# A graph network on one core: column sums of the tail tiles moved into relations, loads moved into the choice, w2 scaled earlier

## The reference

```python
x = x + _L1_gnn_ref(_layernorm(x), L1_gnn_weight, edge_weight1, src, dst, edge_type_16)
x = x + _L1_ffn_ref(_layernorm(x)[None], Wr, br, W1, b1, W2, b2, gamma, beta)[0]
```

```python
logits = jnp.mean(x, axis=1) @ Wr + br          # x: the normed rows, mean over all 6250
... softmax, capacity scale, softmax, top_k(2), softmax of the two
out = w_a * y_a + w_b * y_b                     # y_e = gelu(x W1_e + b1_e) W2_e + b2_e
out = _layer_norm(out + x, gamma, beta)
```

## Time and profile before

| | |
|---|---|
| median of three executions | 3174.28 us (3172.42 to 3178.28) |
| the profiled execution | 3175.51 us, span 3173.8 us |
| mean granted TensorE clock | 0.886 of full speed |
| TensorE busy | 2449.2 us, 77% |
| VectorE busy | 1760.3 us, 55% |
| GpSimd busy | 1947.8 us, 61% |
| ScalarE busy | 850.3 us, 27% |

### The profile page before, as it was taken

One profiled execution on the slowest core, in us unless ns is written; L12 is line 12 of the kernel. 1 busy time (PEld: TensorE's weight loads), 2 busy tenths in 40 slices (PEclk: granted clock), 3 DMA queues, 4 the chain that ended last, 5 costly groups with the idle time before them and its releaser, 6 DMA issues. The chain is left out here.

```text
span 3173.8 us, 37270 instructions
## 1 busy us (share of the span) xinstructions
PE 2449.2 (77%) x8964; PEld 1576.1 (50%) x8964; DVE 1760.3 (55%) x4135; ACT 850.3 (27%) x1683; POOL 1947.8 (61%) x1900
## 2 busy tenths in 40 slices
PE   4537999999999999999979918999999300004897
PEld 3425566656665666565546505666666200003565
DVE  6776555555556666666640046665555544543664
ACT  2211333333333333333223303333333100002221
POOL 6477555646666777778830057777777777760443
PEclk9767999999999999999989958999999755555999
DMA  7553544445445555555531374555554433332210
GB/s 251 119 172 89 152 136 129 142 148 146 139 143 158 150 148 159 168 159 150 147 98 67 111 257 145 157 152 169 155 156 142 124 105 104 106 98 86 77 56 29
DMA packets 241629, 428.29 MB, mean 135 GB/s; under 512 B 49866, under 2 KB 132418, under 8 KB 241538
## 3 DMA queue, kind: packets, MB, share of 16 engines
q0 software_dynamic: 84608, 232.41, 27.6%
q1 hardware_dynamic: 131250, 171.29, 15.8%
q10 hardware_dynamic: 25680, 23.60, 2.2%
HBM read 271.16 MB, written 155.97 MB: 135 GB/s over the span
## 5 line engine op out<-in xcount | busy, mean ns | idle before, releaser
L810 POOL DMA_INDIRECT gat_rows<-h_table,idx x799 | 901.4, 1128 | 424.5 <-issue 231.3
L1437 POOL DMA_INDIRECT rel_rows<-transformed,rel_idx x799 | 756.0, 946 | 475.3 <-issue 466.5
L1054 PE MATMUL bank<-tr_wr,tr_xt 128*128 128x512 f32 x1568 | 724.0, 600 | 39.1 <-ACT tr_row L903 34.3
L1054 PEld LDWEIGHTS bank<-tr_wr,tr_xt 128*128 128x128 f32 x1568 | 293.4, 191 | 328.9 <-issue 277.6
L1019 PE MATMUL bank<-mo_xt,mo_w 128*128 128x256 f32 (+1 forms) x1600 | 431.8, 393 | 15.2 <-ACT mo_ht L894 13.5
L1626 DVE SCALAR_TENSOR_TENSOR bank<-rel_rows,rel_now,bank 128x256 f32<-128x256 f32 x823 | 403.1, 490 | 40.3
L903 ACT ACTIVATE tr_row<-bank 128x512 f32<-128x512 f32 x392 | 233.8, 597 | 675.8 <-PE bank L1054 662.6
L1037 PE MATMUL bank<-mo_w,mo_ht 128*128 128x256 f32 x1568 | 369.3, 381 | 4.5 <-ACT mo_ht L894 4.5
L1019 PEld LDWEIGHTS bank<-mo_xt,mo_w 128*128 128x128 f32 x1600 | 286.9, 192 | 148.0 <-issue 101.4
L1209 DVE TENSOR_TENSOR gat_rows<-gat_rows 128x1024 f32<-128x1024 f32 (+1 forms) x169 | 254.5, 1529 | 156.2 <-DVEq L1200 156.2
L1037 PEld LDWEIGHTS bank<-mo_w,mo_ht 128*128 128x128 f32 x1568 | 299.1, 191 | 55.5 <-issue 11.0
(11 more groups left out here) (295 smaller groups left out, 2342.2 us busy)
## 6 DMA issues: line engine op xcount, KB each, us to landing
transformed<-tr_row SPq DMA_DIRECT2D x392, 256.0 KB, 2.2
ys<-ex_y ACTq DMA_DIRECT2D x160, 128.0 KB, 2.2
gat_rows<-h_table,idx POOLq DMA_INDIRECT x799
rel_rows<-transformed,rel_idx POOLq DMA_INDIRECT x799
ex_w<-L_ffn_W SPq DMA_DIRECT2D x16, 512.0 KB, 12.2
h_table<-hrow SPq DMA_DIRECT2D x49, 132.0 KB, 2.4
records<-xa SPq DMA_DIRECT2D x49, 132.0 KB
x_moved<-tr_x SPq DMA_DIRECT2D x24, 256.0 KB, 3.2
```

The costliest lines, as they stand in the source:

```text
L810: pool.indirect_dma_start(out=rows[:, column(u, j), :], out_offset=None, in_=p.h_table[:], in_offset=bass.IndirectOffsetOnAxis(ap=idx[u][: ...
L1054: ins = pe.matmul(p.bank[6 + c % 2][:], xt2[:, k, u * P:(u + 1) * P], wr[:, k, m * CW:(m + 1) * CW], start=(k == 0), stop=(k == KD - 1))
L1437: pool.indirect_dma_start(out=rows[:, column(u, j), :], out_offset=None, in_=p.transformed[:], in_offset=bass.IndirectOffsetOnAxis(ap=idx[ ...
```

## The change

Three things are moved, and some names and counts follow.

1. The column sums of the tail tiles leave `choose_two` and stand in `relations`, behind TensorE's last group. VectorE signals `rows_done` after every pair of tail tiles and after the last tile (15 signals); TensorE waits for it tile by tile, and at the end for its own `summed_up`. The sums lie in banks 1 and 2 in place of 0 and 1.
2. SP loads gamma and beta and, for the first two done batches, `xd` and `x3` in `choose_two`, and waits there until all six have landed. The buffers are kept ones now. In `feed_forward` the expert weights are issued first, then b2, then only `ye` for these two batches. For later batches `xd` and `x3` are issued ahead of `ye`.
3. `scale` stands ahead of batch 0, behind the two operations on b2.

FREE, REUSED and X_LOADS have the values 9, 29 and 32, so the loads of `rec` in `relations` are the same as before.

```diff
@@ relations, SP, TensorE and VectorE @@
-    FREE = TAIL - DONE
+    FREE = max(TAIL - DONE, 0)
+    REUSED = DONE + FREE
+    X_LOADS = 32 if FREE else 16
...
             group(GROUPS - 1, True)
+            for t in range(TAIL):
+                pe.wait_ge(rows_done, t // 2 + 1)
+                for k in range(KD):
+                    ins = pe.matmul(p.bank[1 + k][:, 0:1], p.rec[:, t, k * P:(k + 1) * P], p.ms[:, DONE + t, 2:3],
+                                    start=(t == 0), stop=(t == TAIL - 1))
+            ins.then_inc(summed_up, 1)
+            pe.wait_ge(summed_up, 1)
...
                 spread_of(i, 2 * i, 2)
+                if tail:
+                    dve.sem_inc(rows_done, 1)
...
             spread_of(PAIRS, NT - 1, 1)
+            dve.sem_inc(rows_done, 1)
@@ choose_two @@
             sp.dma_start(br[:], a["L1_ffn_br"].rearrange("(o e) -> o e", o=1)).then_inc(w_in, 16)
+            for n, name in enumerate(("L1_ffn_gamma", "L1_ffn_beta")):
+                sp.dma_start(p.gb[:, n], bass.AP(tensor=a[name].tensor, offset=0, ap=[[0, P], [1, D]])).then_inc(ahead, 16)
+            for g in range(2):
+                sp.dma_start(p.xd[g][:], p.xn_table.rearrange("(g j q) d -> g q j d", q=P, j=G)[g]).then_inc(ahead, 16)
+                sp.dma_start(p.x3[g][:], p.x_moved.rearrange("(t q) d -> q t d", q=P)[:, g * G:(g + 1) * G, :]).then_inc(ahead, 16)
+            sp.wait_ge(ahead, 16 * 6)
...
-            for t in range(TAIL):
-                for k in range(KD):
-                    ins = pe.matmul(p.bank[k][:, 0:1], p.rec[:, t, k * P:(k + 1) * P], p.ms[:, DONE + t, 2:3],
-                                    start=(t == 0), stop=(t == TAIL - 1))
-            ins.then_inc(summed, 1)
...
-            dve.wait_ge(summed, 2)
+            dve.wait_ge(summed, 1)
@@ feed_forward @@
             for n, e in enumerate(experts):
-                sp.dma_start(b2[:, n], a["L1_ffn_b2"][bass.ds(e, 1)].broadcast_to([P, D])).then_inc(b_in, 16)
-            for n, name in enumerate(("L1_ffn_gamma", "L1_ffn_beta")):
-                sp.dma_start(gb[:, n], bass.AP(tensor=a[name].tensor, offset=0, ap=[[0, P], [1, D]])).then_inc(b_in, 16)
-            for n, e in enumerate(experts):
...
+            for n, e in enumerate(experts):
+                sp.dma_start(b2[:, n], a["L1_ffn_b2"][bass.ds(e, 1)].broadcast_to([P, D])).then_inc(b_in, 16)
...
                         sp.wait_ge(finished, units(b - 1))
+                        sp.dma_start(xd[s][:], xns[g]).then_inc(loaded[s], 16)
+                        sp.dma_start(x3[s][:], moved[:, g * G:(g + 1) * G, :]).then_inc(loaded[s], 16)
                     for n, e in enumerate(experts):
                         sp.dma_start(ye[s][n][:], ys[bass.ds(e, 1), g].rearrange("o q j d -> (o q) j d")).then_inc(loaded[s], 16)
-                    sp.dma_start(xd[s][:], xns[g]).then_inc(loaded[s], 16)
-                    sp.dma_start(x3[s][:], moved[:, g * G:(g + 1) * G, :]).then_inc(loaded[s], 16)
...
-            dve.wait_ge(b_in, 16 * 4)
+            dve.wait_ge(b_in, 16 * 2)
...
-                if b == 1:
+                if b == 0:
                     scale()
```

More of the change, by code:

```diff
@@ L1327, in relations @@
     LOCAL = E1 * F
-    FREE = TAIL - DONE
-    assert DONE % 2 == 0 and FREE >= 0
+    FREE = max(TAIL - DONE, 0)
+    REUSED = DONE + FREE
+    X_LOADS = 32 if FREE else 16
+    assert DONE % 2 == 0
     with p.phase() as ctx:
@@ L1403, in _ @@
             sp.dma_start(beta[:], bass.AP(tensor=a["L1_ffn_beta"].tensor, offset=0, ap=[[0, P], [1, D]])).then_inc(beta_in, 16)
-            sp.dma_start(p.rec[:, FREE:TAIL, :], moved[:, 0:DONE, :]).then_inc(x_in[0], 16)
-            sp.dma_start(p.rec[:, 0:FREE, :], moved[:, DONE:TAIL, :]).then_inc(x_in[0], 16)
+            sp.dma_start(p.rec[:, FREE:REUSED, :], moved[:, 0:DONE, :]).then_inc(x_in[0], 16)
+            if FREE:
+                sp.dma_start(p.rec[:, 0:FREE, :], moved[:, DONE:REUSED, :]).then_inc(x_in[0], 16)
             for e in range(E1):
@@ L1408, in _ @@
                 sp.dma_start(w2[:, e * F:(e + 1) * F, :], a["L1_ffn_W2"][e].rearrange("(f q) d -> q f d", q=P)).then_inc(w_in[2 * e // E1], 16)
-            sp.wait_ge(x_in[0], 32)
+            sp.wait_ge(x_in[0], X_LOADS)
             for t in range(DONE):
@@ L1412, in _ @@
                 sp.dma_start(moved[:, t, :], x3b[t % 2][:]).then_inc(x3_out[t % 2], 16)
-            for g in range(GROUPS):
+            for g in range(-(-(NT - REUSED) // G)):
+                lo, hi = g * G, min((g + 1) * G, NT - REUSED)
                 sp.wait_ge(xn_ready, g + 1)
-                sp.dma_start(p.rec[:, FREE + g * G:FREE + (g + 1) * G, :],
-                             moved[:, TAIL + g * G:TAIL + (g + 1) * G, :]).then_inc(x_in[1], 16)
+                sp.dma_start(p.rec[:, FREE + lo:FREE + hi, :], moved[:, REUSED + lo:REUSED + hi, :]).then_inc(x_in[1], 16)
                 sp.wait_ge(x_in[1], 16 * (g + 1))
-                sp.sem_inc(tail_ready, G)
+                sp.sem_inc(tail_ready, hi - lo)
         @block.gpsimd
@@ L1694, in spread_of @@
                 dve.sem_inc(x3_done, 1)
-            dve.wait_ge(x_in[0], 32)
+            dve.wait_ge(x_in[0], X_LOADS)
             for u in range(2):
@@ L1701, in pair @@
                 if reused:
-                    dve.wait_ge(tail_ready, 2 * i + 2 - TAIL)
+                    dve.wait_ge(tail_ready, 2 * i + 2 - REUSED)
                     p.alone(dve)
@@ L1707, in pair @@
                 spread_of(i, 2 * i, 2)
-            for lo, hi, tail, reused in ((0, DONE // 2, False, False), (DONE // 2, TAIL // 2, True, False), (TAIL // 2, PAIRS, True, True)):
+                if tail:
+                    dve.sem_inc(rows_done, 1)
+            for lo, hi, tail, reused in ((0, DONE // 2, False, False), (DONE // 2, REUSED // 2, True, False), (REUSED // 2, PAIRS, True, True)):
+                if lo == hi:
+                    continue
                 with dve.Fori(lo, hi) as i:
                     pair(i, tail, reused)
-            dve.wait_ge(tail_ready, DONE)
+            dve.wait_ge(tail_ready, NT - REUSED)
             tile(PAIRS, 0, NT - 1, NT - 1 - DONE, True)
             spread_of(PAIRS, NT - 1, 1)
+            dve.sem_inc(rows_done, 1)
             for u in range(2):
@@ L1737, in choose_two @@
                                         "exp_ready", "exp_done", "pair_ready", "spread_done"))
+        ahead = p.sem("two_ahead")
         block = ctx.enter_context(nc.Block())
@@ L1841, in feed_forward @@
         BATCHES.append(("tail", n))
+    assert BATCHES[0] == ("done", 0) and BATCHES[1] == ("done", 1)
     with p.phase() as ctx:
@@ L1876, in units, with landed @@
             return sum(size(*BATCHES[i]) for i in range(b))
-        def loads(b):
-            return sum(1 for i in range(b) if BATCHES[i][0] == "done" and i % 2 == b % 2)
+        def landed(b):
+            return sum(4 if i >= 2 else 2 for i in range(b + 1) if BATCHES[i][0] == "done" and i % 2 == b % 2)
         def loads_of(b):
@@ L1918, in base @@
                     s = b % 2
-                    pool.wait_ge(loaded[s], 16 * 4 * (loads(b) + 1))
+                    pool.wait_ge(loaded[s], 16 * landed(b))
                     for j in range(G):
@@ L2042, in _ @@
                 s, n = b % 2, size(kind, g)
-                if b == 1:
+                if b == 0:
                     scale()
                 if kind == "done":
-                    dve.wait_ge(loaded[s], 16 * 4 * (loads(b) + 1))
+                    dve.wait_ge(loaded[s], 16 * landed(b))
                 for j in range(n):
@@ L2083, in build @@
         attention(p)
-        p.rec = p.keep("rec", [P, TAIL, D], F32)
+        p.rec = p.keep("rec", [P, max(DONE, TAIL), D], F32)
         relations(p)
+        p.gb = p.keep("gb", [P, 2, D], F32)
+        p.xd = [p.keep(f"xd{n}", [P, G, D], F32) for n in range(2)]
+        p.x3 = [p.keep(f"x3{n}", [P, G, D], F32) for n in range(2)]
         choose_two(p)
```

7 lines of the change are left out of this document (3 added, 4 removed).

## The result

The changed kernel takes 3140.68 us (median of 4; 3139.08 to 3144.52), the kernel before 3173.35 (median of 4 on its chips, the three shown above and one more). The ratio is 0.9897, 95% interval 0.988 to 0.9914: 32.7 us faster, with 3144.5 forecast and 3139 to 3151 given as range. The profiled execution took 3144.52 us, the slowest of the four, with a span of 3142.7 against 3173.8: 31.1 us less, with 29.8 forecast. That it took the very time that was forecast for the median is chance. Two of the runs further down hold one execution each, of 5962.09 and 6845.3 us, that stands far outside all others, and their medians are given without it.

The account below looks back on a forecast made before the run. TensorE's tail groups bound the end, behind two holes: column sums standing alone after 385.7 us idle, and a 5.5 us wait for w2. +1.0 - 22.2 - 5.5 - 3.1 = -29.8 us from 3174.28 gives 3144.5, range 3139 to 3151.

Parts of the forecast that it names:

- The sums: End of relations: column sums hide in TensorE's idle time, only the last tile's 4 passes show, +1.0 us.
- I gave it 0.03: Rival in relations: the sums aren't hidden, all 116 passes run in a row after it, 3168.4 us; chance 0.03.
- The choice: Stage choose_two: without the sums, SP's wait for the early loads ends it at 12.0 us; -22.2 us.
- VectorE's part: In the choice: products wait for the small loads wr and br until 2.8, so VectorE ends at about 10.3 us.
- The start of the last stage: Weights issued 2.05 us earlier gain nothing, since TensorE waits for ScalarE's 29 norms and copy of b1.
- Half clock: Start of the last stage: TensorE's half-speed start stays, until about 9 us after its first transposes.
- Scaling and clock: First two groups: early scaling removes the wait for w2, -5.5 us; without that pause the clock stays full, -3.1 us.
- VectorE now scales w2 ahead of batch 0 ... the 5.5 us go: Last stage: scaling ends near 2927 or 2930, TensorE asks at 2945.8, so the second group's wait vanishes, -5.5 us.
- The prefetch did hold the choice: Rival in the choice: early loads move at the slow rate and the choice ends at 16.7, 3149.2 us; chance 0.07.
- the slow case: In the choice: the 2.36 MB move at 181 to 190 GB/s, the choice ends at 16.7 us, gain -17.5; chance 0.07.
- The wait for w2: Rival in the last stage: scaling is delayed past the first group, 5.5 and 3.1 us stay, 3153.1 us; chance 0.04.
- half clock after 385 us: Rival in the last stage: idle TensorE stays at half clock, slower, at most 3354 us; chance 0.02.

Follow-up runs that it names:

- the kernel with 5 norms later: Against the changed kernel, ScalarE norms the last 5 of 29 tail tiles in the first group's time, behind the copy of b1: 3143.2 us, ratio 0.99.
- an experiment of its own: Six useless products on TensorE inside its wait for w2, against the kernel with only the sums moved: 3148.23 us against 3151.62.
- the two kernels that take one part away: Changed kernel with scaling again behind batch 0: 4041.32 and 4035.4 us; with early loads back in the last stage: 4034.05 and 4033.94 us.

## Why the prediction was right, point by point

**The sums.** Forecast +1.0 for the end of relations, measured +1.06 (2.91 against 1.85). That they hide was right on the chip the forecast was made for; the two other chips show a condition that I hadn't weighed: TensorE's expert groups must be through before the last tail tiles are. With 385.7 us to spare I gave it 0.03, which is fair for the chip of the profile and says nothing of a chip on which TensorE itself pauses.

**The choice.** Forecast -22.2, measured 13.12 - 35.47 = -22.35. The loads landed where the two later batches said: by 11.8 us (13.12 less the 1.32 of the barriers) against 12.0. The rule of the Trainium skill that I weighed against them (page "DMA: Bandwidth & Descriptors", section "Anatomy of one DMA — SWDGE (gpsimd) path") would have had them at 8.3, an estimate worked out from its fit, and the choice ended by VectorE; the trace decides against this reading of it. One term was mis-sized, off the path: VectorE's part was 9.69 and not 10.3, because wr and br didn't hold anything. The products with wr, which wait for both loads, started 0.15 us behind VectorE (0.14 before), and 1.96 us after wr's issue, 1.54 after br's, so both had landed by then; the 2.4 us that I took from a 16 KB load were too much for br.

**The start of the last stage.** Forecast nothing, measured 14.47 and 14.47: the norms covered the earlier weights, as the kernel with 5 norms later shows. Half clock: 20.0 us for the first group before, without its wait for w2, and 19.46 after (2923.12 - 2903.66), because the clock rose 8 us after the first transposes and not 9. In stretches (columns as above), 0.62 as the mean of 2911 to 2912 puts the rise a quarter from its end:

```profile
2911.00:2912.00 1.00, 1.00 (x3) 0.37 (x2) 1.00 (x2) 0.38 (x1) 1.00 (x2) 0.62 0.00 0
2922.00:2924.00 2.00, 2.00 (x11) 1.15 (x10) 1.96 (x6) 0.97 (x2) 1.46 (x2) 1.00 0.20 70
```

Over the runs that don't wait for w2 the first group takes between 18.56 and 19.98. That half microsecond was in the range, not in the sum.

**Scaling and clock.** Forecast -5.5 and -3.1, measured: no wait, and 29.87 against 32.85 in the second group. The sizes were right, and the second has an experiment of its own. The step "VectorE now scales w2 ahead of batch 0 ... the 5.5 us go" was right in its sum and wrong in whom it credits: I named both that the scaling moves and that the batches run some 5 us earlier by the loads, and charged the whole gain to the first. Either nearly suffices. On the chip of the forecast this rests on the lengths of the last stage, which are the same on all chips: the two kernels that take one part away ran on the others only.

**The sum.** -29.8 forecast; by these lengths -30.3 (79.83 against 110.09 us from the last copy to the third group), and 0.8 us by which VectorE's last copy happened to come earlier, 31.1 in all. The median went 32.7 down; the rest is the spread between executions, of which the profiled one was the slowest.

**The other rivals.** The prefetch did hold the choice, by 2.1 us where the likeliest case had 1.7, and not by the 6.4 of the slow case. The wait for w2 didn't come back. TensorE didn't stay at half clock after 385 us with next to no work.

## What to carry to other kernels

Work that only needs data arriving bit by bit belongs beside the arrival, on an engine that is idle there; its price is then the last piece, 4 passes here in place of 116, but only while that engine is in fact done with what stands ahead of it in its queue. A load that is put ahead of a barrier must fit under what the stage has to do anyway: here it was 2.1 us too long, and a semaphore that outlives the stage gave the loads early without it. Nor did they buy anything here once the scaling stood ahead of batch 0. When two parts of a change both remove the same wait, take each away alone before crediting either.

## What the runs showed that I hadn't expected

Two of the three chips on which experiments ran took 4050 us for a kernel that takes 3173 to 3175 on the others, with the same median durations of single instructions (592 ns for a pass of L1496 on both kinds; a group of the last stage lasts 29.86 us on all) and with pauses in the earlier stages that the trace puts down to nothing, of up to 28 us before L1496. A change worth 1.0% on one is worth 0.35 to 0.5% on the other. TensorE's stop of 5.5 us took the clock away, and stops of 0.9 and 1.8 us at the same place didn't.
